# Macaron layer: the next group's step sizes and B/C projection six slots sooner, its gate products five slots later

## The reference

```python
x = x + 0.5 * ffn(layernorm(x))
x = x + mamba(layernorm(x))
x = x + 0.5 * ffn(layernorm(x))

def ffn(x):                      # 8 experts of width 176, the best 2 per token; one shared of width 352
    w = scatter(softmax(top2(x @ Wg)))
    y = sum_e w[:, e] * ((silu(x @ W1[e]) * (x @ W2[e])) @ W3[e])
    return y + (silu(x @ Ws1) * (x @ Ws2)) @ Ws3

def mamba(x):                    # 256 inner channels, 16 states, a causal convolution of 4 taps
    x_in, z = split(x @ W_in + b_in)
    xc = silu(conv(x_in) + conv_b)
    B, C = split(xc @ W_xp + b_xp)
    delta = softplus(xc @ W_dt + b_dt)
    h_t = exp(delta_t * A) * h_(t-1) + delta_t * xc_t * B_t;  y_t = sum_states(h_t * C_t)
    y = (y + D_skip * xc) * silu(z)
    return layernorm2(x + y @ W_out + b_out)
```

## Time and profile before

| what | value |
|---|---|
| executions shown | 1890.74, 1891.11, 1896.28 us, median 1891.11 |
| profiled execution: its own time | 1897.91 us |
| profiled execution: span of the trace | 1896.2 us |
| mean granted TensorE clock | 0.956 of full speed |
| PE busy | 1672.0 us, 88% of the span |
| DVE busy | 1543.4 us, 81% |
| POOL busy | 1435.9 us, 76% |
| ACT busy | 1230.4 us, 65% |

### The profile page before, as it was taken

The page is one execution under the profiler, slowest core; times in us unless marked ns, Lnnn a source line. Parts: engine busy times, 40 slices in busy tenths (PEclk is TensorE's granted clock), DMA queues, the critical chain, the costliest instruction groups (busy, mean ns, idle before and its releaser), DMA issues.

```text
span 1896.2 us, 27794 instructions
## 1 busy us (share of the span) xinstructions
PE 1672.0 (88%) x7378; PEld 1004.6 (53%) x7378; DVE 1543.4 (81%) x2337; ACT 1230.4 (65%) x1838; POOL 1435.9 (76%) x1318
## 2 busy tenths in 40 slices
PE   5888788989899998989989998999989898957488
PEld 3454444556565555556555555655555555634255
DVE  1358989899888988989888988989888998988732
ACT  2367677676858676676767676676766767665421
POOL 3346878878888887888888888788878888877753
PEclk9998799999999999999999999999999999979698
DMA  5127667686867778586777767677676868767742
GB/s 157 42 73 169 154 163 193 146 188 158 193 166 173 177 168 188 142 194 167 179 169 166 184 156 185 171 173 183 155 191 148 193 152 192 169 143 188 158 104 67
DMA packets 121344, 305.11 MB, mean 161 GB/s; under 512 B 19300, under 2 KB 40519, under 8 KB 106823
## 3 DMA queue, kind: packets, MB, share of 16 engines
q0 software_dynamic: 18432, 125.84, 33.5%
q1 hardware_dynamic: 98406, 174.46, 32.6%
q10 hardware_dynamic: 4320, 2.71, 0.5%
HBM read 167.67 MB, written 5.24 MB: 91 GB/s over the span
## 4 chain that ended last, share of the span: by engine, by line
PE 34%; DVE 19%; issue 15%; POOL 15%; ACT 8%; DMA 7%; DVEq 1%; ACTq 0%; SPq 0%; POOLq 0%
PE ps_y L1101 9%; DVE hist L927 7%; POOL prod L628 6%; PE ps_h2b L1109 5%; POOL gated L568 5%; PE ps_h1a L1087 5%; PE ps_h1b L1087 4%; DMA yacc<-prod 4%; PE ps_h2a L1109 3%; DVE ps_db L879 3%; DVE gated L907 2%; PE ps_m L1048 2%; ACT decay L691 2%; PE ps_m L1152 2%; DVE yacc L996 1%
## 5 line engine op out<-in xcount | busy, mean ns | idle before, releaser
L628 POOL TENSOR_TENSOR prod<-hist,crow 128x1024 f32<-128x1024 f32 x224 | 556.4, 2484 | 232.1 <-DVE hist L927 227.4
L1101 PEld LDWEIGHTS ps_y<-down_w,gated 128*128 128x128 f32 (+1 forms) x3584 | 471.8, 195 | 287.3 <-issue 156.2
L927 DVE TENSOR_TENSOR_SCAN hist<-decay,ps_db 128x1024 f32<-128x1024 f32 x256 | 583.2, 2278 | 2.8
L568 POOL TENSOR_TENSOR gated<-gated,silu 128x512 f32<-128x512 f32 x352 | 492.3, 1455 | 79.7 <-DVE gated L907 71.2
L1101 PE MATMUL ps_y<-down_w,gated 128*128 128x128 f32 (+1 forms) x3584 | 489.2, 281 | 68.2 <-POOL gated L568 67.1
L879 DVE TENSOR_TENSOR ps_db<-du,ps_db 128x1024 f32<-128x1024 f32 x256 | 313.0, 1222 | 103.9 <-PE ps_db L1069 101.2
L691 ACT ACTIVATE decay<-delta,a_neg 128x510 f32<-128x510 f32 x512 | 326.8, 708 | 5.7 <-DVE delta L970 4.3
L711 ACT ACTIVATE silu<-ps_h1a 128x512 f32<-128x512 f32 (+1 forms) x224 | 133.1, 594 | 257.2 <-PE ps_h1a L1087 256.5
L1087 PE MATMUL ps_h1a<-xnT,up_w 128*128 128x512 f32 (+1 forms) x448 | 238.7, 614 | 10.7 <-issue 10.7
L1087 PE MATMUL ps_h1b<-xnT,up_w 128*128 128x512 f32 x448 | 238.9, 615 | 5.2 <-ACT silu L711 4.7
L1109 PE MATMUL ps_h2b<-xnT,up_w 128*128 128x512 f32 x448 | 237.2, 612 | 1.7 <-DVE gated L907 1.7
(11 more groups left out here) (139 smaller groups left out, 1946.4 us busy)
## 6 DMA issues: line engine op xcount, KB each, us to landing
yacc<-prod POOLq DMA_DIRECT2D x112, 1024.0 KB, 10.0
crow<-c_rows SPq DMA_DIRECT2D x128, 512.0 KB, 5.0
wrow<-w_rows SPq DMA_DIRECT2D x320, 128.0 KB, 6.4
wrow<-w_rows SPq DMA_DIRECT2D x64, 224.0 KB, 7.0
wrow<-w_rows SPq DMA_DIRECT2D x64, 192.0 KB, 4.5
wrow<-w_rows SPq DMA_DIRECT2D x64, 160.0 KB, 3.0
yacc<-yacc POOLq DMA_DIRECT2D x16, 512.0 KB, 7.7
wrow<-w_rows SPq DMA_DIRECT2D x64, 96.0 KB, 3.2
```

Of the source, the lines that this page charges most:

```text
L568: nc.gpsimd.tensor_tensor(gated[:, pos % NGATE, :], gated[:, pos % NGATE, :], silu[:, (pos + NCHUNK * f_parity(of, f)) % NSILU, :], ALU.mu ...
L628: nc.gpsimd.tensor_tensor(prod[:, (pair - 1 + odd) % 2, s % 2, :, :], hist[:, s % 2, :, :], c_all, ALU.mult).then_inc(prod_done, 1)
L927: nc.vector.tensor_tensor_scan(hist[:, s % 2, :, :].rearrange("p h t -> p (h t)"), decay[:, s % NA, :, :, :].rearrange("p h b t -> p (h b ...
L1101: ins = nc.tensor.matmul(ps_y[:, t * C:(t + 1) * C], gated[0:rd, posd % NGATE, t * P:(t + 1) * P], down_w[0:rd, jd, :], start=(posd == 0 a ...
```

## The change

The three tables are edited, and nothing else. In `PLAN`, `dt0` and `dt1` move from slots 17 and 18 to 14 and 15; `sp_exp` and `xproj` from 20 to 16; `bparts` from 22 to 16; `sp_ln` from 22 to 18; `delta` from 26 to 20; `du` from 28 to 22. `in2` and `in3` go from 14 and 15 to 19 and 21. `wT0` goes from 16 to 17. In `UNIT` the second FFN's chunk 12 starts in slot 16 and not 15. In `SP_PLAN` `store_w0` and the first four `w0` fetches all stand in slot 18, ahead of `c6`.

```diff
-        11: ["resid", "route0"], 12: ["stats3", "in1a", "tilt0"], 13: ["in1", "scale3"], 14: ["in2", "ln_norm", "weights0"],
-        15: ["in3", "ln_scale"], 16: ["wT0", "ln_shift"], 17: ["dt0"], 18: ["dt1", "ln_add"], 19: ["stats1"],
-        20: ["sp_exp", "xproj", "scale1"], 21: ["addy1"], 22: ["norm1", "sp_ln", "bparts"], 23: ["xT1"], 24: ["logits1"],
-        25: ["rcopy1", "route1"], 26: ["cT", "delta"], 27: ["bT", "tilt1"], 28: ["weights1", "du"], 30: ["wT1"],
+        11: ["resid", "route0"], 12: ["stats3", "in1a", "tilt0"], 13: ["in1", "scale3"], 14: ["dt0", "ln_norm", "weights0"],
+        15: ["dt1", "ln_scale"], 16: ["sp_exp", "xproj", "bparts", "ln_shift"], 17: ["wT0"], 18: ["sp_ln", "ln_add"],
+        19: ["in2", "stats1"], 20: ["delta", "scale1"], 21: ["addy1", "in3"], 22: ["norm1", "du"], 23: ["xT1"],
+        24: ["logits1"], 25: ["rcopy1", "route1"], 26: ["cT"], 27: ["bT", "tilt1"], 28: ["weights1"], 30: ["wT1"],
...
-    UNIT = {s: (1, pos) for pos, s in enumerate((0, 1, 2, 3, 4, 5, 6, 7, 8, 10, 12, 14, 15, 17))}
+    UNIT = {s: (1, pos) for pos, s in enumerate((0, 1, 2, 3, 4, 5, 6, 7, 8, 10, 12, 14, 16, 17))}
...
-        11: ["c4"], 12: ["w1:10"], 15: ["c5"], 17: ["store_w0", "w0:0", "w0:1"], 18: ["w0:2"], 19: ["c6", "w0:3"],
+        11: ["c4"], 12: ["w1:10"], 15: ["c5"], 18: ["store_w0", "w0:0", "w0:1", "w0:2", "w0:3"], 19: ["c6"],
```

## The result

The changed kernel took **1951.62 us** (median of 4 runs, 1950.55 to 1956.38) where the kernel before took 1891.89 beside it: a ratio of 1.0307, 95% interval 1.0288 to 1.0325. The forecast was 1870, the high end of its range 1903; the prediction was wrong in sign. The profiled execution has a span of 1954.6 us and a mean granted clock of 0.941 (before: 0.956).

A forecast was written before the change was run, and what follows sets the result against it. A loop body was taken to last as long as PE's work plus PE's waits. A saving of 1.75 us in each of 12 bodies made 21 us, so 1891.1 became 1870 us, with a range of 1852 to 1903.

The forecast's parts named there:

- I take 1.2 (POOL's current instruction is a join or its like): Slot 16: `brem` would take 1.2 us, waiting for POOL's current instruction, so `wT0` on PE waits 0.2.
- The upper bound beside it: Slot 16: `brem` takes at most 4.5 us, to the end of the `prod` that starts at 1026.05.
- rival 3: Slot 16: `brem` held through POOL's whole stretch, `wT0` waits 3.3 us; 12 to 30 us slower, 1903 to 1921; chance 0.17.
- If they get in between ... I take the first: Slot 25: routing's two small instructions get in between POOL's; scan some 0.85 us early, otherwise 0.15 late.
- rival 1: Slot 25: the routing instructions lose against `prod`; gain only 0.75 us a body, 9 us, giving 1882; chance 0.20.
- the gain in slot 22 that I counted for DVE: Slot 22: `du` replaces the split; DVE gains 2.4 us, less 0.7 for the later row of B, so 1.6.
- `dt1` waits 1.36 in each body: Slots 14 to 15: PE stands still about 1.36 us ahead of `dt1`, in place of 0.5, while ACT reads `dt0`.
- xT1's wait is gone: Slots 22 to 24: PE's 1.40 us wait for `brem` ahead of `xT1` goes, leaving PE 0.8 early.
- Rival 2: First FFN's gates: routing weights arrive late by DMA, leaving nothing of the gain at two us; about 1888; chance 0.15.
- PE's wait in slot 29: Down product of slot 29: PE's wait for POOL's join falls from 2.35 to 1.4 us.
- 1.75 early: Slots 25 to 29: the join comes 0.85 + 0.9 = 1.75 us early, and PE leaves slot 29 that much early.
- The sign of a join's wait of over 1 us in slot 21: Sign of being right: the last down product of slot 21 waits for a join by over 1 us.

The follow-up runs named there:

- yield_hot: The changed kernel, with POOL waiting for the routing's `hot` ahead of the `prod` of state 12; 1909.61 us, 1.0064 of the kernel before.
- split_psum: The changed kernel, with sums and rest of B written to PSUM so no split instruction reads two SBUF tensors; 1904.87 us, 1.0051 of the kernel before.
- split_psum_hot: The changed kernel, with the split of B by way of PSUM and POOL waiting for `hot` ahead of state 12's `prod`; 1877.41 us, 0.9914 of the kernel before.
- dma_gap: The changed kernel, with POOL doing and awaiting a single-column instruction behind each DMA it issues; 1932.95 us, 1.0205 of the kernel before.
- before_dma_gap: The kernel before, with POOL doing and awaiting a single-column instruction behind each DMA it issues; ratio 1.0169 to the kernel before.

## Why the prediction was wrong

**The step that failed first** is "I take 1.2 (POOL's current instruction is a join or its like)". The upper bound beside it was right, 4.5 us until the `prod` of state 8 ends, and so was the condition for it, a gate behind `brem` that POOL needs. `brem` took 4.52 in all twelve bodies, and `wT0` waited 3.27, where rival 3 had said 3.3. I chose by the row in which `du` "did get in after two"; I did not ask what POOL did just then: behind the second of those joins stood only `prob`, the last of its stretch, and POOL paused for 0.08 us behind that (1065.90 + 1.49 to `hotp` at 1067.47). The price of rival 3, 12 to 30 us, was low: taking `brem`'s wait away gave back 2.3%, 44 us.

**The second** is "If they get in between ... I take the first", of the routing instructions. I saw that POOL would be late there, and counted their losing as against one `prod`, 0.15 us a body. `drop` lost against the rest of a join, a `prod` and two more joins, and yield_hot gave back 2.4%, 46 us. So rival 1 came with rival 3, at 46 us and not at the 12 that lay between my 21 and the 9 I had left to it. And the gain in slot 22 that I counted for DVE, 1.6, was itself the cause: with scan 12 2.2 us sooner behind scan 11, POOL's wait of 1.67, which had let `drop` in, was gone. That wait stands in no line of my working.

The Trainium skill ("SBUF — State Buffer", section "SBUF: two separate sides") says that GpSimd and a VectorE instruction with two SBUF inputs exclude each other, whoever starts first having the pair for its whole instruction. split_psum agrees about the inputs (0.23 us from PSUM against 4.52), but for the waiting time the measurement decides: 4.52 is the rest of a join and two whole instructions, 8.96 six.

**What held.** `dt1` waits 1.36 in each body (16.3 in 12). xT1's wait is gone. `du` takes 1.20, the `prod` of state 11 3.26, that of state 13 2.36, all as in the text. Rival 2 did not come: gates waited for the DMA of the routing weights twice in the loop, 2.5 us in all, although the store of body 8 went out only at 1061.43; its first fetch followed 1.47 later and not 2.8. With the two instructions freed (split_psum_hot) the sum came out at 0.9%, where the forecast had 1.1%.

**What agreed by luck, or not at all.** PE's wait in slot 29 is 1.45 in body 8, and the forecast was 1.4:

```profile
1100.15 1.16 PE L1101 MATMUL ps_y<-down_w,gated 128*128 128x128 f32 x8 [1.45 <-POOL gated L568]
```

But the join there came late and not 1.75 early: this product starts 3.8 us later behind the body's first scan than before, and in six of the twelve bodies its wait is under 0.2. Even in split_psum_hot that wait lies anywhere between 0 and 1.45, so the total came out nearer than the path to it. The sign of a join's wait of over 1 us in slot 21 failed in the change: it is 0.87 in two loop bodies and under 0.1 in the others. In split_psum_hot it is there, 1.29 to 1.32 in all twelve, so that part of the working held once `brem` was freed.

**What was not asked** is whether the kernel before would gain the same from less.

## What to carry to other kernels

Before a DVE instruction with two SBUF operands is moved, look at POOL at the new place, not for how busy it is but for whether each instruction starts 0.3 us ahead of the end of the last, as here behind a DMA that POOL issued. There, count the wait to POOL's next pause, not to the end of the current instruction. Then mend the place and not the order: one operand in PSUM, or a wait of POOL on its own last result just ahead, which cost 0.1 to 0.2 us here. An idle stretch of another engine can be the door by which a third instruction comes in, so a step that removes it has to be charged for that.

## What was not expected of the hardware

POOL's instructions run in two ways. Worked out from the rows of fourteen traces (both kernels and the runs without dma_gap and before_dma_gap), taking a start over 0.1 us ahead of the end of the instruction before as early: all 1467 stretches of early starts begin directly behind a DMA that POOL issues, and all but 13 last until POOL stands idle. Arithmetic DVE instructions of two SBUF operands were passed over at 344 ends of POOL's computing instructions (an end counts where the DVE record goes on for more than the instruction takes alone), each of which had itself started early; not once at the end of one that had not, though POOL went on at once there in 157 cases. One case fits only in part: 69 times `du` came in at the end of a join although the short `prob` behind it, the last of its stretch, had started early; `prob` then lasted longer (1.49 us before, against 0.50 in after). In dma_gap and before_dma_gap, where POOL waits behind each issue, the only early starts left are the 128 of the added instruction in each trace. Early starts bring POOL nothing: in after its instructions follow each other by 1.23 us (1053.55, 1054.78, 1056.02), in dma_gap, without them, by 1.24 (1043.42, 1044.66, 1045.90); the record of one is longer by what it starts sooner (1.59 against 1.28). Why an issue sets this off, no run here shows.
